# A Mamba block with linear attention: one scan unit in four driven by TensorE, the convolution as diagonal matmuls

## What is computed

```python
# block 0, Mamba with modulation by c
xn = layernorm(x) * (1 + scale) + shift              # ada = silu(c) @ ada_w.T + ada_b
x_in, z = split(xn @ in_proj_w.T)                    # 512 channels each
u = silu(causal_conv(x_in, conv_w, 4 taps) + conv_b)
dt_r, B, C = split(u @ x_proj_w.T, [64, 80])         # B, C: 16 states each
dt = softplus(dt_r @ dt_proj_w.T + dt_proj_b)
h = h * exp(dt * A) + dt * u * B                     # for each step, 512 x 16 states
y = sum over states of h * C + u * D_param
x = x + gate * ((y * silu(z)) @ out_proj_w.T)
# block 1, linear attention, 8 heads of 32
q, k, v from layernorm(x);  q = softmax over a head, k = softmax over time (masked)
y = q @ (k^T v);  hh = layernorm(y) * (1 + scale1) + shift1
out = x + silu(hh) @ W_out + b_out
```

## Time and profile before

| | us |
|---|---|
| median of 3 runs | 666.56 |
| lowest, highest | 663.95, 671.63 |
| the profiled execution | 668.15 |
| its span, first to last instruction | 666.3 |

### The profile page before, as it was taken

The page is one execution under the profiler, slowest core; times in us unless marked ns, Lnnn a source line. Parts: engine busy times, 40 slices in busy tenths (PEclk is TensorE's granted clock), DMA queues, the critical chain, the costliest instruction groups (busy, mean ns, idle before and its releaser), DMA issues.

```text
span 666.3 us, 7102 instructions
## 1 busy us (share of the span) xinstructions
PE 452.1 (68%) x2352; PEld 376.6 (57%) x2352; DVE 589.3 (88%) x618; ACT 405.9 (61%) x874; POOL 389.4 (58%) x292
## 2 busy tenths in 40 slices
PE   3848687678566756778567856776666956775764
PEld 3637566566465645666456745665665756654642
DVE  4809999999999999999999999999999999999321
ACT  2374756558655868387755866487737774754232
POOL 4066759547855786557845694657746696661100
PEclk9978876898689789889689778989789966877886
DMA  7273042002400070005200160007000240000000
GB/s 214 70 248 122 1 162 92 1 16 78 178 1 0 19 268 1 0 17 179 92 0 13 50 226 1 0 16 260 12 0 1 82 190 0 1 16 1 0 16 17
DMA packets 19870, 44.31 MB, mean 67 GB/s; under 512 B 2348, under 2 KB 11060, under 8 KB 19829
## 3 DMA queue, kind: packets, MB, share of 16 engines
q1 hardware_dynamic: 19832, 43.84, 18.9%
HBM read 41.48 MB, written 2.36 MB: 66 GB/s over the span
## 4 chain that ended last, share of the span: by engine, by line
DVE 58%; issue 14%; PE 11%; ACT 9%; POOL 6%; DMA 1%; DVEq 0%; SPq 0%; ACTq 0%; POOLq 0%
DVE ring L635 33%; DVE hs L639 8%; DVE conv L625 5%; POOL hs L383 4%; PE YT L940 3%; ACT ring L504 3%; PE PY L983 2%; DVE st L605 2%; DVE yt L646 2%; DVE kmax L682 2%; PE PX L901 1%; ACT L455 1%; PE PX L836 1%; PE PY L1024 1%; ACT L578 1%
## 5 line engine op out<-in xcount | busy, mean ns | idle before, releaser
L383 POOL TENSOR_TENSOR hs<-dtu,BC 128x1024 f32<-128x1024 f32 x128 | 299.7, 2358 | 107.8 <-PE YT L940 107.7
L635 DVE TENSOR_TENSOR_SCAN ring<-ring,hs 128x1024 f32<-128x1024 f32 x128 | 292.1, 2282 | 20.2 <-POOL hs L383 16.2
L504 ACT ACTIVATE ring<-dt,Aneg 128x256 f32<-128x256 f32 x512 | 213.2, 464 | 149.2 <-DVE hs L639 149.1
L940 PE MATMUL YT<-ident,hs 128*128 128x128 f32 x1024 | 160.0, 312 | 51.5 <-DVE hs L639 51.4
L940 PEld LDWEIGHTS YT<-ident,hs 128*128 128x128 f32 x1024 | 139.9, 163 | 67.6 <-DVE hs L639 62.5
L639 DVE TENSOR_TENSOR hs<-ring,BC 128x1024 f32<-128x1024 f32 x128 | 156.8, 1225 | 4.4
L901 PE MATMUL PX<-xnT,win 128*128 128x256 f32 x232 | 67.0, 439 | 27.2 <-ACT xnT L435 11.2
L901 PEld LDWEIGHTS PX<-xnT,win 128*128 128x128 f32 x232 | 48.8, 222 | 39.9 <-ACT xnT L435 13.6
L983 PE MATMUL PY<-wqkvo,xT 128*128 128x256 f32 x192 | 63.3, 489 | 0.0
L983 PEld LDWEIGHTS PY<-wqkvo,xT 128*128 128x128 f32 x192 | 49.5, 258 | 10.2
L362 POOL TENSOR_TENSOR dt<-dt,conv 128x512 f32<-128x512 f32 x16 | 20.3, 1271 | 53.0 <-ACT conv L484 53.0
(11 more groups left out here) (126 smaller groups left out, 601.4 us busy)
## 6 DMA issues: line engine op xcount, KB each, us to landing
BC<-bc_rows SPq DMA_DIRECT2D x32, 1024.0 KB, 10.1
xg<-in_x SPq DMA_DIRECT2D x8, 256.0 KB, 2.8
out<-fin SPq DMA_DIRECT2D x8, 256.0 KB, 12.3
BC<-in_ada_wT SPq DMA_DIRECT2D x3, 512.0 KB, 5.0
win<-in_in_wT SPq DMA_DIRECT2D x2, 512.0 KB, 6.7
BC<-in_W_emb SPq DMA_DIRECT2D x2, 512.0 KB
wo<-in_out_wT SPq DMA_DIRECT2D x1, 512.0 KB, 13.0
bc_rows<-xdbl SPq DMA_DIRECT2D x8, 32.0 KB, 1.5
```

Of the source, the lines that this page charges most:

```text
L383: nc.gpsimd.tensor_tensor(hs[:, g % DBUF], dtu[:, b % 2, dc, :].unsqueeze(1).to_broadcast([P, NQ, T]), BC[:, b % 2, NQ * q:NQ * q + NQ, :] ...
L504: ins = nc.scalar.activation(ring[:, g % 2, j, :], dt[:, b % 2, dc, :], ACT.Exp, scale=Aneg[:, c:c + 1])
L635: V.tensor_tensor_scan(states, states, driven, 0.0, ALU.mult, ALU.add).then_inc(s_scan_done, 1)
L940: ins = M(YT[:, c, :], hs[:, g % DBUF, j, P * c:P * c + P], ident[:, :], is_transpose=True, start=False, stop=(q == UPC - 1 and j == NQ - ...
```

## The change

Every fourth unit (q = 3, `by_pe`) is driven otherwise: PE makes dtu * B as a matmul of the transposed dtu (`transpose_dtu`, ACT copies it to dtuT) with a diagonal matrix of B (`diagonals`, POOL, from BT, which x_proj now also gives) into ring in PSUM (`drive`, in the pass before the unit); ACT writes its decays to da in SBUF; DVE scans da and ring into hs; POOL multiplies hs by C (`states_times_c`, two passes later). Three units in four stay as they were. The convolution becomes 16 matmuls a batch with diagonals of conv_w (`convolve`); ACT copies x_in in (`copy_x`) and the result out with its bias (`copy_u`). The skip term becomes a matmul of u with a diagonal of D. z is projected with time on the partitions, so that `gate_y` multiplies YT by it for each chunk in place of the copy, before PE turns it back (`transpose_yg`) and ACT copies it (`copy_yg`). The sums of q are narrow matmuls in k_times_v, the reduction negates kmax itself. gate comes by DMA, out is stored from x1, sum_states runs two passes later (LAG). B and C have tiles and DMAs of their own. Most slots change.

```diff
-DBUF, XBUF = 5, 3
+XBUF, HBUF, ABUF = 3, 5, 1
+LAG = 2
+PE_QUARTERS = (3,)
+BEHIND = 2
...
+def by_pe(g):
+    return g % UPC in PE_QUARTERS
+def by_pool(g):
+    return by_pe(g)
...
@@ build @@
+        diagW = sb("diagW", [P, DC * TAPS, P])
+        diagD = sb("diagD", [P, DC, P])
-        BC = sb("BC", [P, 2, 2 * N, T])
-        hs = sb("hs", [P, DBUF, NQ, T])
+        dtuT = sb("dtuT", [P, 2, TC, DI])
+        diagB = sb("diagB", [P, 2, TC, NQ, P])
+        Br = sb("Br", [P, 2, N - NQ * len(PE_QUARTERS), T])
+        Cr = sb("Cr", [P, 2, N, T])
+        da = sb("da", [P, ABUF, NQ, T])
+        hs = sb("hs", [P, HBUF, NQ, T])
...
@@ GpSimd @@
+            def setup_diags():
+                pool.wait_ge(s_ld_par, 32)
+                pool.wait_ge(s_ld_ident, 16)
+                for h in range(2):
+                    lo = DC * TAPS // 2 * h
+                    nc.gpsimd.tensor_tensor(
+                        diagW[:, lo:lo + DC * TAPS // 2, :], ident[:, :].unsqueeze(1).to_broadcast([P, DC * TAPS // 2, P]),
+                        pcol("conv_w", lo, lo + DC * TAPS // 2).unsqueeze(2).to_broadcast([P, DC * TAPS // 2, P]),
+                        ALU.mult).then_inc(s_diags, 1)
+                nc.gpsimd.tensor_tensor(
+                    diagD[:, :, :], ident[:, :].unsqueeze(1).to_broadcast([P, DC, P]),
+                    pcol("D_par").unsqueeze(2).to_broadcast([P, DC, P]), ALU.mult).then_inc(s_diags, 1)
...
+            def diagonals(b):
+                pool.wait_ge(s_BT_ready, b + 1)
+                if b >= 2:
+                    pool.wait_ge(s_dbu_mm, pe_driven(U * (b - 1)))
+                nc.gpsimd.tensor_tensor(
+                    diagB[:, b % 2], ident[:, :].unsqueeze(1).unsqueeze(1).to_broadcast([P, TC, NQ, P]),
+                    BT[:, b % 2].unsqueeze(3).to_broadcast([P, TC, NQ, P]), ALU.mult).then_inc(s_diagB_ready, 1)
...
+            def states_times_c(b, i):
+                g, q = U * b + i, i % UPC
+                pool.wait_ge(s_scan_done, g + 1)
+                if i < UPC:
+                    pool.wait_ge(c_loaded[b % 2][q], 16 * (b // 2 + 1))
+                nc.gpsimd.tensor_tensor(hs[:, g % HBUF], hs[:, g % HBUF], Cr[:, b % 2, NQ * q:NQ * q + NQ, :],
+                                        ALU.mult).then_inc(s_hc_pool, 1)
...
             for g in range(FIRST, LAST):
-                if 0 <= g < NB * U:
+                if 0 <= g < NB * U and not by_pe(g):
                     inputs_of(g // U, g % U)
-                for slot, step in ((-17, rstd0), (-3, softplus_0), (-1, softplus_1), (24, residual), (26, rstd1),
-                                   (38, rstd2)):
+                if 0 <= g - BEHIND < NB * U and by_pool(g - BEHIND):
+                    states_times_c((g - BEHIND) // U, (g - BEHIND) % U)
+                if g == -20:
+                    setup_diags()
+                for slot, step in ((-21, rstd0), (-7, softplus_0), (-5, softplus_1), (-4, diagonals),
+                                   (21, residual), (23, rstd1), (33, rstd2)):
...
@@ ScalarE @@
-            def conv_last_tap(b, h):
+            def copy_x(b, h):
                 act.wait_ge(s_xz_mm, 4 * b + h + 1)
-                if b >= 1:
+                if b == 0:
+                    act.wait_ge(s_pool_const, 9)
+                else:
                     act.wait_ge(s_dt_sum, 2 * b)
+                nc.scalar.activation(vln[:, 2 * h:2 * h + 2, :], xz_bank(b, h)[:, :, :], ACT.Copy).then_inc(s_xin_ready, 1)
+            def copy_u(b, h):
+                act.wait_ge(s_conv_mm, 2 * b + h + 1)
+                if b >= 2:
+                    act.wait_ge(s_y_acc, U * (b - 2) + U - UPC + 1)
                 for e in range(2):
                     dc = 2 * h + e
+                    ins = nc.scalar.activation(u[:, b % 2, dc, :], conv_bank(b, h)[:, e, :], ACT.Identity,
+                                               bias=pcol("conv_b", dc, dc + 1))
+                ins.then_inc(s_uraw_ready, 1)
...
+                if by_pe(g):
+                    k = pe_driven(g)
+                    dst = da[:, k % ABUF]
+                    if k >= ABUF:
+                        act.wait_ge(s_scan_done, pe_unit(k - ABUF) + 1)
+                else:
+                    dst = ring[:, g % 2]
+                    if g >= 2 and by_pool(g - 2):
+                        act.wait_ge(s_scan_done, g - 1)
+                    elif g >= 2:
+                        act.wait_ge(s_hc_dve, dve_units(g - 1))
+                    else:
+                        act.wait_ge(s_z_ready, 2)
                 for j in range(NQ):
                     c = N * dc + NQ * q + j
-                    ins = nc.scalar.activation(ring[:, g % 2, j, :], dt[:, b % 2, dc, :], ACT.Exp,
-                                               scale=Aneg[:, c:c + 1])
+                    ins = nc.scalar.activation(dst[:, j, :], dt[:, b % 2, dc, :], ACT.Exp, scale=Aneg[:, c:c + 1])
...
-                for slot, step in ((-17, normalize0), (-16, modulated), (-15, conv_last_tap_0), (-14, conv_last_tap_1),
-                                   (-11, copy_z), (-6, copy_xdbl), (-5, softplus_parts_0), (-3, softplus_parts_1),
-                                   (25, normalize1), (26, norm1), (30, exp_qk), (31, mask_v), (32, copy_qT),
-                                   (33, copy_kT), (38, normalize2)):
+                for slot, step in ((-18, normalize0), (-17, modulated), (-16, copy_x_0), (-15, copy_x_1),
+                                   (-14, copy_u_0), (-13, copy_u_1), (-11, copy_z), (-7, copy_xdbl),
+                                   (-6, softplus_parts_0), (-5, softplus_parts_1), (-3, copy_dtuT_0), (-2, copy_dtuT_1),
+                                   (18, copy_yg_0), (19, copy_yg_1), (25, normalize1), (26, norm1), (29, exp_qk),
+                                   (30, mask_v), (31, copy_qT), (32, copy_kT), (36, normalize2)):
...
@@ VectorE @@
             def scan_unit(b, i):
-                g = U * b + i
-                q = i % UPC
+                g, q = U * b + i, i % UPC
                 dve.wait_ge(s_da_ready, g + 1)
-                dve.wait_ge(s_dbu_ready, g + 1)
-                driven = hs[:, g % DBUF].rearrange("p n t -> p (n t)")
-                states = ring[:, g % 2].rearrange("p n t -> p (n t)")
-                V.tensor_tensor_scan(states, states, driven, 0.0, ALU.mult, ALU.add).then_inc(s_scan_done, 1)
-                dve.wait_ge(s_scan_done, g + 1)
-                if i < UPC:
-                    dve.wait_ge(bc_loaded[b % 2][q], 16 * (b // 2 + 1))
-                V.tensor_tensor(hs[:, g % DBUF], ring[:, g % 2], BC[:, b % 2, N + NQ * q:N + NQ * q + NQ, :],
-                                ALU.mult).then_inc(s_hc_ready, 1)
+                if by_pe(g):
+                    k = pe_driven(g)
+                    dve.wait_ge(s_dbu_mm, k + 1)
+                    if g >= HBUF:
+                        dve.wait_ge(s_y_acc, g - HBUF + 1)
+                    decays, driven = flat(da[:, k % ABUF]), flat(ring[:, g % 2])
+                else:
+                    dve.wait_ge(s_dbu_pool, pool_driven(g + 1))
+                    decays, driven = flat(ring[:, g % 2]), flat(hs[:, g % HBUF])
+                states = flat(hs[:, g % HBUF]) if by_pool(g) else flat(ring[:, g % 2])
+                V.tensor_tensor_scan(states, decays, driven, 0.0, ALU.mult, ALU.add).then_inc(s_scan_done, 1)
+                if not by_pool(g):
+                    dve.wait_ge(s_scan_done, g + 1)
+                    if i < UPC:
+                        dve.wait_ge(c_loaded[b % 2][q], 16 * (b // 2 + 1))
+                    V.tensor_tensor(hs[:, g % HBUF], ring[:, g % 2], Cr[:, b % 2, NQ * q:NQ * q + NQ, :],
+                                    ALU.mult).then_inc(s_hc_dve, 1)
+            def gate_y(b, dc):
                 dve.wait_ge(s_y_acc, U * b + UPC * (dc + 1))
+                dve.wait_ge(s_z_ready, 2 * b + 2)
+                z = zs[:, b % 2, :, P * dc:P * dc + P]
+                V.tensor_tensor(z, YT[:, :, :], z, ALU.mult).then_inc(s_ygT_ready, 1)
...
-                V.tensor_reduce(kmax[:, :], PZ[:, :, :], AX.X, ALU.max).then_inc(s_kmax_ready, 1)
+                V.tensor_reduce(kmax[:, :], PZ[:, :, :], AX.X, ALU.max, negate=True).then_inc(s_kmax_ready, 1)
...
+                V.reciprocal(rq[:, :, :].rearrange("p c h -> p (c h)"), PZ[:, 1, 0:TC * HEADS]).then_inc(s_qrec_ready, 1)
...
-                for slot, step in ((-23, stats0), (-16, conv_taps_0), (-14, conv_taps_1), (19, gate_y), (21, gate_x),
-                                   (22, stats1), (27, max_qk), (29, sums_qk), (32, head_blocks), (33, normalize_q),
-                                   (34, stats2), (40, finish)):
+                for slot, step in ((-22, stats0), (21, gate_x), (22, stats1), (27, max_qk), (29, sum_k),
+                                   (31, head_blocks), (32, normalize_q), (33, stats2), (40, finish)):
...
@@ TensorE @@
+            def convolve(b, h):
```

(82 more changed lines are left out.)

447 lines of the change are left out of this document (226 added, 221 removed).

## The result

The changed kernel takes 764.82 us (median of 4 runs, 763.37 to 766.96), the kernel before, on the same chip, 669.1 (4 runs, 663.95 to 672.19): a ratio of 1.144, 95% interval 1.138 to 1.150. The sign was right, the time is 30 us above the forecast of 735, at the top of the range of 695 to 765, and above the 718 to 755 that the prediction gave for the forecast without its rivals. The profiled execution took 763.37 for a span of 761.6.

The account below looks back on a forecast made before the run. POOL's order was taken as the bound: 59.4 of DVE work, 17.8 of POOL's waits, 2.5 for kv and 1.2 for gate_x make 81 us a middle batch; 59 + 72 + 6 x 81 + 70 + 49 = 736 of span; forecast 735, range 695 to 765.

Parts of the forecast that it names:

- POOL's order: POOL waits at steps placed too early, then owes DVE the next input; 17.8 us a batch on DVE.
- kv before head_blocks: DVE stands at head_blocks because kv on PE waits for ACT's copy_kT; 2.5 us a batch.
- the half clock: PE at 1.2 GHz after some 6 us idle before slot 13; kv 2.4 us later, only in the range's upper half.
- Batch 0: First batch, with softplus, rstd0, diagonals and emb's setup product ahead of the second convolution on PE; 72 us.
- DVE's list: DVE's work in a middle batch falls by 13.0 us, from 72.4 to 59.4.
- softplus_0: POOL's step for which the input of unit 10 comes late; costs DVE 4.8 us a batch.
- gate_x: DVE's gate_x waits for out_proj behind the long part of PE's work; about 1.2 us a batch, at least 0.
- PE's list: PE's work a batch grows by 18.4 us; PE busy some 65 to 68 us a batch.
- A: Rival: work lists decide, not the order; once POOL's waits cost under 11, batch 63 us, total 610; chance 0.13.
- B: Rival: POOL's waits alone, those for kv and gate_x hidden by them; 77.2 us a batch, total 707; chance 0.2.
- C: Rival: PE at half clock from slot 13 until kv, another 6 us at head_blocks; batch 87, total 774; chance 0.07.
- D: Rival: waits near 11 us a batch cancel the 13 saved less what start and edges lose; total 668; chance 0.04.

Follow-up runs that it names:

- both_later: Changed kernel with POOL's steps behind the scan later, and those ahead of it moved too (DVE's stats0 earlier): 670.9 us, 1.005 of the kernel before.
- Experiments 1 to 3: Changed kernel with slots moved for POOL's steps behind the scan, those ahead of it (with DVE's stats0, PE's transpose_dtu_0), then both: 719.33, 718.35, 670.9 us.
- experiment 6: Changed kernel with 12 extra matmuls, work for nothing, in PE's gap behind slot 12: 752.04 us, 1.130 of the kernel before.
- experiment 5: Changed kernel with PE's setup product for emb in slot 5 instead of 0, DVE's gate8 and emb steps five slots later: 758.55 us, 1.141 of before.

## Why the prediction was right in its mechanism and too low in its sum

The mechanism, POOL's order, was right. The steps that failed are terms of the sum. The wait for kv before head_blocks was put at 2.5 us a batch without the half clock of PE, and was 4.39 to 4.75 in five of the six middle batches. The wait for the drive of unit 15 was put at nothing, and was 0.72. Batch 0 was put at 72, and took 83.5. That the time still lies at the top of the stated range owes something to the start, which came 3.7 earlier than forecast.

- **DVE's list** (forecast 59.4 us a middle batch): 59.7 busy, 60.5 with its short pauses. Scans with an operand moved take 2270 ns on average, the others 2290. The value left at 2.32 from a scan to what follows holds for the others; a moved scan has no multiplication behind it, and the next instruction mostly starts after 2.2, the lower bound given.
- **POOL's order** (17.8 a batch): 17.6, unit by unit (forecast, measured): rstd2 3.6, 3.65; residual 3.3, 3.15; rstd1 1.6, 1.99; softplus_0 4.8, 4.72 in two parts; rstd0 with softplus_1 2.5, 2.88; diagonals 1.2, 0.60; multiplication by C 0.8, and 0.64 at the gate_y beside it. The diagonals took 1.90, not an input's 2.36. One name is off: of the 4.8 at unit 10, 2.51 stand at gate_y, where PE's sums wait behind dt_proj_1 for ACT's softplus. It adds nothing here, since POOL's input for unit 10 is not done before the end of the 4.72 anyway; in both_later, without POOL's delay, 0.81 of it shows. So 14.5 of the 17.6 name POOL in the trace, just under the 15 to 18 that were to show it. Experiments 1 to 3 show these waits to be the cause, 94 us of it.
- **kv before head_blocks** (2.5): 4.73. The mechanism was there and the order of the terms too, but the half clock after PE's gap, which I priced at 2.4 and then left "only in the upper half of my range", belonged in the sum: the gap was forecast as "some 6 us" and was 5.81. In experiment 6 the wait falls to 2.71, 0.2 from my 2.5, in the three middle batches of five in which both slow stretches go, and to 4.04 and 3.77 in the two in which kv stays at half clock. This is the mis-sized term of the middle batches, and the half clock is shown for up to 2.0 of it.
- **gate_x** (1.2): 1.57, and 0.18 at the gate_y behind it. Not in the sum at all: 0.72 for the drive of unit 15, again PE at half clock (2.24), 0.21 at normalize_q, and 0.8 in pauses under 0.15. With 0.3 of work, a batch of 85.5 where 81 stood.
- **Edges.** The six middle batches took 503.3 instead of 486, 17.3 of the 25.6 us by which the span is longer than the sum of 736. Batch 0 took 83.5 instead of 72, 11.5 more; the start 55.3 instead of 59, the last batch 69.5 (70), the end 50.0 (49). Of batch 0's error 4.4 are two small DVE instructions that no row of the trace suggested there, though rows 5 had one of their kind (L682, 1476 ns for two columns); the other 7.1 lie in DVE's waits, some 25 us in all there, of which the longest is for the drive of unit 3, 10.3 us. I had priced none of them singly, only put 72 where the kernel before took 67.1; experiment 5 moved this wait rather than taking it away, so what it costs by itself stays open.
- **PE's list** (65 to 68 busy): 69.2 with the stretches at half clock. The narrow records came as estimated: 16 of 4 columns in 1.84 us at x_proj, 8 of them in 1.05 before kv, so 0.115 to 0.13 with the group's end. On the price by weight columns alone, the Trainium skill ("TensorE: Matmul & The Clock Gate", Part 2, LDWEIGHTS) and this trace agree.
- **Rivals.** A put the batch at 63 once POOL's waits cost less than 11. In both_later they cost nothing and the batch is 72.2; the best order found gives 66.4. What A missed is that PE's list, too, is worked off in order and has its own waits: 63 would want PE full in every quarter. B had the right POOL waits, but none of the two others were hidden by them. C had the right clock and place at three times its price or more: between its two stretches at 1.2 GHz PE was back at 2.4 GHz, and experiment 6 puts what it took away at head_blocks at 2.0 of C's 6 us in the batch shown. D's batch wasn't seen.
- **The start of the argument**, that DVE bounds the kernel before and that lists of work say little about the kernel after, held: the changed kernel has less to do on every engine than its time by 16 us or more a batch.

## What to carry to other kernels

Where every engine works off a fixed order, a shorter list on the bound engine is worth nothing until the order has been mended for it: first move each step that waits on another engine behind that engine's step by as many units as the producer is ahead (here moves of one or two slots, most of them on POOL, gave 94 us, and one slot too many on DVE and POOL cost 23). Price the half clock into the sum wherever the forecast itself says that TensorE stands idle. And after the order is mended, ask again which list is the longest: here work taken from DVE had been given to PE, whose list became the longest (62.9 us of a batch of 67.4, DVE's 58.7), and work taken from it in one place shortened the batch.
